# Moving the second gating product of each expert tile from VectorE to GpSimd

## What is computed

```
# first mixture, per expert e (D 512, F 192, two experts per token)
g = einsum('btd,edf->ebtf', x, gate_w)
u = einsum('btd,edf->ebtf', x, up_w)
h = silu(g) * u
expert_out = einsum('ebtf,efd->ebtd', h, down_w)
# scan, per step
state = state * exp(d * A) + (d * u) * b
y = einsum('bdn,bn->bd', state, c)
```

## Time and profile before

| what | value |
|---|---|
| median of three runs | 1677.16 us (1675.82 to 1680.13) |
| the profiled execution, its own time | 1682.74 us |
| span of the profiled execution | 1680.6 us |
| mean granted clock of TensorE | 0.89 |
| busy share PE / DVE / POOL / ACT | 83% / 58% / 45% / 40% |

### The profile page before, as it was taken

One profiled execution on the slowest core, in us unless ns is written; L12 is line 12 of the kernel. 1 busy time (PEld: TensorE's weight loads), 2 busy tenths in 40 slices (PEclk: granted clock), 3 DMA queues, 4 the chain that ended last, 5 costly groups with the idle time before them and its releaser, 6 DMA issues.

```text
span 1680.6 us, 19467 instructions
## 1 busy us (share of the span) xinstructions
PE 1400.6 (83%) x6048; PEld 1034.9 (62%) x6048; DVE 971.6 (58%) x1258; ACT 664.8 (40%) x1223; POOL 757.2 (45%) x551
## 2 busy tenths in 40 slices
PE   6988980645898699789535599999999999999998
PEld 4534440634565466556324488787878787878786
DVE  2768669899898699689698223223232324242322
ACT  4435441244564366356312233333333333333332
POOL 0000004366686488468362144445454545454543
PEclk9799885566998899799866599999999999999999
DMA  3211226005777978887464760001000100010000
GB/s 99 102 53 48 101 77 225 29 16 186 254 238 234 315 234 253 273 284 236 158 213 176 249 255 13 0 0 63 13 0 0 62 0 12 0 50 0 0 0 25
DMA packets 75375, 191.15 MB, mean 114 GB/s; under 512 B 10600, under 2 KB 13448, under 8 KB 73792
## 3 DMA queue, kind: packets, MB, share of 16 engines
q1 hardware_dynamic: 62016, 157.03, 27.8%
q0 software_dynamic: 6400, 20.98, 4.3%
q10 hardware_dynamic: 6912, 12.59, 2.0%
HBM read 152.55 MB, written 38.01 MB: 113 GB/s over the span
## 4 chain that ended last, share of the span: by engine, by line
PE 62%; DVE 17%; issue 8%; DMA 7%; POOL 2%; ACT 2%; SPq 2%; ACTq 0%; DVEq 0%; POOLq 0%
PE decay L1644 21%; PE bank L1633 20%; DVE decay L1177 8%; DMA WGU<-in_L_ffn_up_w 6%; PE bank L1520 4%; PE bank L1436 3%; PE decay L1392 2%; PE bank L1495 2%; PE bank L1538 1%; PE bank L1399 1%; POOL Y L715 1%; PE bank L1456 1%; PE decay L1446 1%; PE decay L1442 1%; PE bank L1478 1%
## 5 line engine op out<-in xcount | busy, mean ns | idle before, releaser
L1349 DVE CAST HFH<-HF 128x512 fp32r<-128x512 f32 x128 | 59.0, 461 | 497.9 <-ACT HF L974 497.9
L761 POOL TENSOR_TENSOR W2L<-W2R,W2H 128x512 fp32r<-128x512 f32 x128 | 172.5, 1347 | 348.7 <-ACT W2H L969 348.7
L675 POOL TENSOR_TENSOR S<-DTU,Bb 128x1024 f32<-128x1024 f32 x128 | 299.6, 2362 | 66.0 <-PE bank L1495 49.9
L1177 DVE TENSOR_TENSOR_SCAN decay<-decay,S 128x1024 f32<-128x1024 f32 x128 | 292.9, 2288 | 1.5 <-ACT decay L838 1.5
L1633 PE MATMUL bank<-XSH,W1H 128*128 128x512 f32 x512 | 203.1, 397 | 4.2 <-POOL W1L L757 4.2
L1644 PE MATMUL decay<-W2H,HFH 128*128 128x512 f32 x512 | 200.4, 391 | 5.3 <-DVE HFL L1351 5.3
L1633 PE MATMUL bank<-XSH,W1L 128*128 128x512 f32 x512 | 203.0, 397 | 0.0
L1633 PE MATMUL bank<-XSL,W1H 128*128 128x512 f32 x512 | 202.5, 395 | 0.0
L1644 PE MATMUL decay<-W2L,HFH 128*128 128x512 f32 x512 | 199.9, 390 | 0.0
L1644 PE MATMUL decay<-W2H,HFL 128*128 128x512 f32 x512 | 199.7, 390 | 0.0
L757 POOL TENSOR_TENSOR W1L<-W1R,W1H 128x512 fp32r<-128x512 f32 x128 | 171.0, 1336 | 56.0 <-ACT W1H L962 56.0
(11 more groups left out here) (207 smaller groups left out, 1968.1 us busy)
## 6 DMA issues: line engine op xcount, KB each, us to landing
WGU<-in_L_ffn_gate_w SPq DMA_DIRECT2D x48, 384.0 KB
WGU<-in_L_ffn_up_w SPq DMA_DIRECT2D x48, 384.0 KB
WD<-in_L_ffn_down_w SPq DMA_DIRECT2D x48, 384.0 KB, 3.8
Bb<-bc_rows SPq DMA_DIRECT2D x32, 512.0 KB, 8.7
Cb<-bc_rows SPq DMA_DIRECT2D x32, 512.0 KB, 8.7
expert_rows<-YT ACTq DMA_DIRECT2D x48, 256.0 KB
W1R<-in_L_ffn_w SPq DMA_DIRECT2D x8, 1024.0 KB, 13.9
W2R<-in_L_ffn_w SPq DMA_DIRECT2D x8, 1024.0 KB, 14.2
```

Of the source, the lines that this page charges most:

```text
L675: pool.tensor_tensor(S[j][:], DTU[:, ds(b, 1), c, :].to_broadcast([P, PAIR, L]), Bb[j][:], ALU.mult).then_inc(dbu_ready, 1)
L761: pool.tensor_tensor(W2L[f % 2][:], W2R[:, ds(e, 1), f, :].rearrange("p e d -> p (e d)"), W2H[f % 2][:].bitcast(F32), ALU.subtract).then_i ...
L1177: dve.tensor_tensor_scan(flat, flat, S[j][:].rearrange("p i l -> p (i l)"), 0.0, ALU.mult, ALU.add).then_inc(scan_done, 1)
```

## The change

The second gating product of a tile is made by POOL. POOL can't read PSUM, so ACT first copies half of the up values into `HH`, ahead of its tanh, and POOL multiplies `HH` by `TG` in place. In POOL's step n the two S products are now those of units 2n+2 and 2n+3; behind them stands `finish_h` of tile n+1, and behind that the gather of tile n+2. Two S products and the first `finish_h` are put ahead of the loop, behind the first two gathers. DVE's step ends with the readout.

```
@@ gpsimd
+            def finish_h(j0, n):
+
+                pool.wait_ge(uh_ready, j0 + (n + 1))
+                pool.wait_ge(gg_ready, j0 + (n + 1))
+                pool.tensor_tensor(HH[n % 2][:], TG[n % 2][:], HH[n % 2][:], ALU.mult).then_inc(hh_ready, 1)
+
             def mixture_steps(b, last):
 
+                j0 = b * NS - NS
                 for n in range(NS):
-                    for u in (2 * n, 2 * n + 1):
-                        dbu(b, u // NP, u % NP)
+                    for u in (2 * n + 2, 2 * n + 3):
+                        if u < UB:
+                            dbu(b, u // NP, u % NP)
+                        elif not last:
+                            dbu(b + 1, 0, u - UB)
+                    if n + 1 < NS:
+                        finish_h(j0, n + 1)
+                    elif not last:
+                        finish_h(j0 + NS, 0)
                     if n + 2 < NS:
                         gather(b * NS - NS, n + 2)
                     elif not last:
@@
             gather(0, 0)
             gather(0, 1)
+            dbu(1, 0, 0)
+            dbu(1, 0, 1)
+            finish_h(0, 0)
@@ scalar
             def tanh_g(j0, n):
                 act.wait_ge(up_ready, j0 + (n + 3))
+                act.activation(HH[n % 2][:], UP[:, F:2 * F], ACT.Copy, scale=0.5).then_inc(uh_ready, 1)
                 act.activation(TG[n % 2][:], UP[:, 0:F], ACT.Tanh, scale=0.5).then_inc(tg_ready, 1)
@@ vector
-            def finish_h(j0, n):
-
-                dve.wait_ge(gg_ready, j0 + (n + 1))
-                dve.scalar_tensor_tensor(HH[n % 2][:], TG[n % 2][:], 0.5, UP[:, F:2 * F], ALU.mult,
-                                         ALU.mult).then_inc(hh_ready, 1)
-
@@ vector, mixture_steps
                     read_out(b, 2 * n + 1)
-                    if n + 1 < NS:
-                        finish_h(j0, n + 1)
-                    elif not last:
-                        finish_h(j0 + NS, 0)
 
             gate_h(0, 0)
-            finish_h(0, 0)
```

More of the change, by code:

```diff
@@ L363, in build_program @@
         gated = sem("gated")
+        uh_ready = sem("uh_ready")
         gt_ready = sem("gt_ready")
```

## The result

The changed kernel took 1980.78 us (median of 4 runs, 1978.0 to 1983.36) beside 1678.64 us for the kernel before in the same measurement: ratio 1.177, interval 1.174 to 1.181. The forecast was 1972 us. The profiled execution of the changed kernel has a span of 1977.1 us, 296.5 more than before.

What follows compares the result with a forecast made beforehand. No engine was full over the whole span, PE leading with 83%; DVE was nearly full in smooth expert tiles. The stage at 699.1 us against 404.1 gave 1682.7 + 295.0 - 5.6 = 1972 us, range 1850 to 2035.

Steps and rivals of the forecast that it cites:

- The order on POOL: On POOL the gather of tile n+2 queues behind the wait for tile n+1's gate, so PE waits at turn_x.
- Wait leg: From the end of up to turn_x, through copy, tanh, gate, product and gather: 6.40 us, about 5.5 of it PE idle.
- The signal to POOL: Hand-over from DVE's gate to POOL's product, an estimated 0.03 us.
- The landing: From the gather's indirect DMA, counted from its start, to its rows in XG: 3.9 us, between 3.2 and 8.2.
- PE leg: From turn_x through add_states, down, turn_h and up to the end of up: 6.25 us at full clock.
- The loss to the clock: PE's work behind each idle stretch runs at the slow clock: 2.23 us a tile more, between 1.7 and 2.6.
- Sum: Period of 14.88 us in 46 tiles, two tiles at 7.30: stage 699.1 us against 404.1, +295.0 us; chance 0.62.
- What was said to stay covered: Weights, Bb and Cb, POOL's S products (4.7 us) and DVE's 7.04 us a tile cost nothing; WGU waits given back.
- Rival (a): Same chain in the expert tiles, but PE's clock holds: period 12.65 us, +192.4, 1869 us; chance 0.22 shared with partial clock falls.
- Rival (b): Same chain, PE's clock never recovers: period 18.9 us, +480, 2157 us; chance 0.10, shared with prices beyond the bounds.
- Rival (c): Gather stays hidden if its path is under add_states' 0.87 us: 4 to 12 us faster, 1665 to 1673 us; chance 0.04.
- Rival (d): POOL's product is never waited for and DVE's gain is lost to WGU: no change, 1677 us; chance 0.02.

Runs made afterwards that it cites:

- the filling: Changed kernel with 40 needless transposes of the identity ahead of PE's wait for XG in every tile: 1927.97 us, ratio 1.145 to the kernel before.
- the ceiling run: Kernel before without the second product at all, PE transposing TG, up half left out of the result: 1670.25 us, ratio 0.994.
- the lead restored: Changed kernel with the gather of tile n+3 at the head of POOL's step n, that of tile 2 ahead of the first product: 1681.77 us, ratio 1.0004.

## Why the prediction was right

The order on POOL was the decisive step and it is shown three ways: moving the gather to the head of POOL's step gives back 295 of 302 us, moving it ahead of the product alone about two thirds, and the wait without the product keeps 95% of the slowdown. Term by term, with the averages over the 46 tiles of the trace whose gather stands behind a gate:

- **Wait leg** 6.40 forecast, 6.88 measured. The copy took its 0.22 (717.01 to 717.24 in the tile shown), the gate its 0.35, the gcol copy its 0.18, and the 0.62 ahead of the indirect DMA came as taken (0.77 in the first two blocks, 0.27 in the last). From tanh to gate it was 0.48 and not 0.36, because in three tiles DVE came late by 1.5 to 2.7 us. POOL's product took 0.59 us and not 0.71: the fixed part of 0.33 us, drawn from two larger sizes, was too big. The estimate of 0.42 us by the Trainium skill, GPSIMD Engine Reference, section 3.1, was 0.17 too low. The signal to POOL was 0.15 and not 0.03 (717.95 to 718.10). The landing, forecast as the median of 3.9, was the term that missed most: the median was 3.8, but a leg that is paid 46 times wants the mean, and that was 4.2, raised by gathers of 5 to 6.6 us near the start of the stage and the ends of the blocks. Counting it from the start of the indirect DMA was right: turn_x follows 0.04 us behind the landing. The 2.6 us worked out from the Trainium skill, DMA: Bandwidth & Descriptors, "Anatomy of one DMA", lies below even the quickest of the 48 (3.3): the trace does not agree with it.
- **PE leg** 8.48 forecast with the clock, 8.04 measured. The loss to the clock was 1.79 us a tile, not 2.23: I took it from an up behind the gap, and here turn_x, add_states and down stand there. The forecast that ups would stay near 2.8 us held.
- **Sum**: the two errors, +0.48 and -0.44, cancel (14.92 against 14.88 us, from the end of one up to the end of the next). That is luck; the range of 1850 to 2035 was what the working could promise.
- **What was said to stay covered** did: PE's long waits in the stage were for XG, and the WGU waits went.

Rival (a), a clock that holds, was wrong by the tables by stretch and by the filling. Rival (b) was wrong: the clock came back in every tile, since no up took more than 2.85 us. Rival (c) had the right price for the gain, 4 to 12 us, as the ceiling run shows with 12 us, and the wrong condition for it: even with the gather hidden the split product spends it. Rival (d) was wrong for this change, but with the lead restored its time is the one that came.

## What to carry to other kernels

Before putting a wait into an engine's queue, list what is issued behind it. A prefetch that was early only because nothing held its engine loses that lead at once, and its whole latency joins the loop, however small the work that was moved. Price such a latency by its mean over the stage, bursts included, and add what TensorE's clock takes behind each idle stretch; and measure the ceiling (leave the moved work out altogether) before tuning the move: here it was 0.6%.

## What was not expected of the hardware

A DVE product of two SBUF operands is held while POOL makes its S products. The 128x192 product took 0.35 to 0.40 us in the 37 of 48 cases that met none of them, and 5.2 to 5.6 us in 9, each of those up to the end of POOL's pair of S products. The product of the kernel before, with one operand in PSUM, took 0.344 us on average, though 19 of its 48 overlap an S product. It is another DVE operation, but DVE's readouts, the same operation with one operand in PSUM, didn't slow beside the same POOL work either (1.23 us at most in 128), which points to the operands and not to the operation. The cost was 3.3% of the kernel. The Trainium skill, GPSIMD Engine Reference, section 1, names this pairing as contention (DVE instructions with two SBUF inputs); the runs agree, and add that the hold lasts over two POOL instructions in a row. In the records of those 9 the DVE product begins 0.3 to 0.7 us before the first S product, while POOL's indirect DMA of the gather runs, so by the records (rough for POOL) it was held although it came first; why, the traces don't show. In the other direction POOL's products kept their 2.36 us.

Work added to an idle engine made the changed kernel 53 us faster, and the groups behind the idle stretch, back at their times of full clock, show that it was by its clock.
